# Attention's column input read from row-order images by strided matmul operands, instead of a second, column-order copy written by the first convolution

## What is computed

```python
B, H, W, C = (16, 56, 56, 64); NH = 8; KD = C // NH
x = x + dwconv3x3(x, pos_w, pos_b)
y = layernorm(x, ln1_g, ln1_b)
q = y @ q_w + q_b;  k = (y @ k_w + k_b) * KD ** -0.5;  v = y @ v_w + v_b
lepe = dwconv5x5(v, lepe_w, lepe_b)
attn_w = softmax(einsum('bhqnd,bhknd->bhnqk', qh, kh) + mask_w)     # along each image row
vw = einsum('bhnqk,bhknd->bhnqd', attn_w, vh)
attn_h = softmax(einsum('bqwnd,bkwnd->bwnqk', qh, kh) + mask_h)     # along each image column
out = einsum('bwnqk,bknwd->bqwnd', attn_h, vw)
x = x + (out + lepe) @ out_w + out_b
x = x + gelu(layernorm(x, ln2_g, ln2_b) @ fc1_w + fc1_b) @ fc2_w + fc2_b
```

## Time and profile before

| | |
|---|---|
| median of three runs | 2081.37 us |
| the profiled execution | 2082.95 us; its span 2081.2 us |
| first convolution | 0 to 297 us of the span |
| attention, rows; columns | 297 to about 935; to about 1535 us |
| second convolution; MLP | about 1535 to 1775; to 2081 us |
| busy, share of the span | PE 89%, PE weight loads 74%, DVE 69%, ACT 60%, POOL 53% |
| DMA | 346.85 MB, mean 167 GB/s |

### The profile page before, as it was taken

How to read it: one execution, slowest core, us unless ns; L and a number is a source line. 1 busy time by engine, 2 the same in 40 slices (tenths; PEclk the granted TensorE clock), 3 DMA queues, 4 the chain that set the end, 5 groups by cost and what they waited for, 6 DMA issues and landing times. The chain is left out here.

```text
span 2081.2 us, 89304 instructions
## 1 busy us (share of the span) xinstructions
PE 1844.1 (89%) x34510; PEld 1546.4 (74%) x34510; DVE 1432.1 (69%) x2285; ACT 1251.9 (60%) x2126; POOL 1111.3 (53%) x1904
## 2 busy tenths in 40 slices
PE   5887427999999999998999999999977886699998
PEld 5887424888887888876877878878867886577776
DVE  3698965777777777766776767767641655688885
ACT  4688754555555555564555555555543667588887
POOL 5357454555455554554555555545543001699997
PEclk8988756999999999999999999999988998799999
DMA  8689747778887787887777777777759995565553
GB/s 136 109 201 232 208 152 178 177 172 181 179 182 170 175 180 171 178 183 172 180 181 175 180 178 179 182 171 181 177 77 148 181 211 175 128 138 135 137 136 82
DMA packets 661155, 346.85 MB, mean 167 GB/s; under 512 B 562462, under 2 KB 613406, under 8 KB 660878
## 3 DMA queue, kind: packets, MB, share of 16 engines
q1 hardware_dynamic: 627782, 298.69, 66.7%
q0 software_dynamic: 31936, 43.83, 7.1%
q10 hardware_dynamic: 1160, 0.13, 0.0%
HBM read 105.42 MB, written 102.76 MB: 100 GB/s over the span
## 5 line engine op out<-in xcount | busy, mean ns | idle before, releaser
L917 ACT ACTIVATE att_prob<-att_st_ps 128x448 f32<-128x448 f32 x896 | 487.0, 544 | 436.9 <-PE att_st_ps L825 436.8
L993 DVE TENSOR_REDUCE att_mm<-att_s_ps 128x8 bf16<-128x448 f32 x896 | 555.9, 621 | 269.1 <-PE att_s_ps L795 265.6
L838 PEld LDWEIGHTS att_pv_ps<-att_vx,att_prob 128*56 128x56 f32 x14336 | 562.3, 132 | 88.0 <-ACT att_prob L917 4.7
L838 PE MATMUL att_pv_ps<-att_vx,att_prob 128*56 128x18 f32 x14336 | 514.6, 202 | 5.2 <-ACT att_prob L917 3.3
L687 POOL DMA_DIRECT2D att_mvt<-att_mneg x256 | 135.8, 535 | 559.1 <-ACT att_mneg L906 476.0
L820 PE MATMUL att_st_ps<-att_mvt,set_both 122*56 122x448 bf16 x1792 | 345.9, 357 | 15.4 <-DMA att_mvt<-att_mneg 14.7
L795 PE MATMUL att_s_ps<-att_kx,att_q_unit 120*56 120x448 bf16 x1792 | 347.4, 360 | 6.9 <-DMA att_q_unit<-att_qk_hi 4.2
L825 PE MATMUL att_st_ps<-att_qx,att_k_hi 128*56 128x448 bf16 x1792 | 344.8, 356 | 0.0
L825 PE MATMUL att_st_ps<-att_qx,att_k_lo 128*56 128x448 bf16 x1792 | 342.4, 353 | 0.0
L678 POOL DMA_DIRECT2D att_qx<-att_q_hilo x512 | 245.1, 487 | 6.0 <-DMA att_q_hilo<-att_qk_lo 4.3
L900 ACT ACTIVATE att_qk_hi<-att_pj,set_bias 128x392 bf16<-128x392 f32 x256 | 150.2, 587 | 124.7 <-PE att_pj L753 124.6
(11 more groups left out here) (213 smaller groups left out, 3161.4 us busy)
## 6 DMA issues: line engine op xcount, KB each, us to landing
att_xt<-xn_chunks SPq DMA_DIRECT2D x128, 196.0 KB
att_k_hi<-att_qk_hi SPq DMA_DIRECT2D x128, 196.0 KB, 3.4
att_qx<-att_q_hilo POOLq DMA_DIRECT2D x512, 49.0 KB
att_k_lo<-att_qk_lo SPq DMA_DIRECT2D x128, 196.0 KB, 3.9
pos_x<-in_x_dram SPq DMA_DIRECT2D x128, 105.0 KB
lepe_x<-v_scratch SPq DMA_DIRECT2D x128, 105.0 KB, 4.4
x_scratch<-pos_x SPq DMA_DIRECT2D x128, 98.0 KB
xn_chunks<-pos_xrt SPq DMA_DIRECT2D x16, 784.0 KB, 5.2
```

What stands on the lines that cost most here:

```text
L838: ins = pe.matmul(pv_ps[v % 2][64 * h:64 * h + L, at:at + 18], prob[t % 4][:, 4 * h + a, :], vx[v][:, VW * j + 36 * a + 18 * h:VW * j + 36 ...
L917: act.activation(out, src, ACT.Exp).then_inc(exp_done, 1)
L993: dve.tensor_reduce(mm[v % 2][:, NH * j:NH * j + NH], s_ps[j % 2][:, 0:S8].rearrange("p (s k) -> p s k", k=L), AX.X, ALU.max).then_inc(max ...
```

## The change

Four things are changed.

1. The first convolution writes no column-order copy: `xct`, its four DVE copies and its store per image are gone. The four row copies of an image are split: ACT makes the first two (`ACT_G = 2`), DVE the other two (`row_copy(n, g)`), where the column copies stood. `hl` has three buffers instead of two.
2. Attention's columns load row-order images: four DMAs of 196 KB fill an image `xi` (two buffers), the DMAs of an image are issued nine and ten chunks ahead in the SP stream (before: five and six), and `project` reads 7 columns of the image as an operand of 56 runs of 7 elements, 56 elements apart. The projection then lies in PSUM with the token's place in its column outermost, so `high` and `low` read PSUM with a step of 7 elements, and write as before.
3. SP's stream of attention is written out instead of looped.
4. At attention's start `load_x(i, 3)` goes ahead of the queries' copies on SP, and on POOL the clearing of the second `qx` goes ahead of filling the first.

The diff, cut:

```diff
+        xi = [sb(f"xi{u}", [128, H, W], BF16) for u in range(2)]
...
+        def by_line(i, t):
+            if i.rows:
+                return t[:, 0:HALF].rearrange("p (l q) -> p l q", q=L)
+            return t[:, 0:HALF].rearrange("p (q l) -> p l q", q=L)
...
+                wait(sp, v_proj, cnt(p, pv, 1, 1))
+                sp.dma_start(xt[u][:, :], x_d[4 * i.at + v]).then_inc(xt_in[u], 16)
+            def load_image_rows(i, v):
+                u = i.at % 2
+                if i.at >= 2:
+                    sp.wait_ge(qk_proj, cnt(Image(i.at - 2, False), 3, 2, 2))
+                sp.dma_start(xi[u][:, LINES * v:LINES * v + LINES, :].rearrange("p l q -> p (l q)"),
+                             x_d[4 * i.at + v]).then_inc(xi_in[u], 16)
+            def load_ahead(i, v, d):
+                near, far = chunk(i, v, d), chunk(i, v, d + 4)
+                if near[0].rows:
+                    load_x(*near)
+                if not far[0].rows and is_there(*far):
+                    load_image_rows(*far)
...
-            loop(sp, body, first)
+            straight(sp, body, first)
...
-                x = xt[v % 2][:, HALF * th:HALF * th + HALF]
+                if i.rows:
+                    x = xt[v % 2][:, HALF * th:HALF * th + HALF].rearrange("p (a b) -> p a b", b=PAIRS)
+                else:
+                    first_line = LINES * v + PAIRS * th
+                    x = xi[i.at % 2][:, :, first_line:first_line + PAIRS]
...
-                act.activation(qk_hi[w][:, at:at + HALF], pj[th][:, 0:HALF], ACT.Identity,
+                act.activation(qk_hi[w][:, at:at + HALF].rearrange("p (l q) -> p l q", q=L), by_line(i, pj[th]), ACT.Identity,
...
-        HL = 2 if pos else 3
+        HL = 3
+        ACT_G = G // 2 if pos else G
...
-                for g in range(G):
+                for g in range(ACT_G):
                     s, jj = g // 2, g % 2
                     act.wait_ge(tr_done, G * n + g + 1)
...
+            def row_copy(n, g):
+                s, jj = g // 2, g % 2
+                if n >= 2:
+                    dve.wait_ge(xr_out[n % 2], 16 * (n // 2))
+                dve.wait_ge(tr_done, G * n + g + 1)
+                rows = xrt[n % 2][:, :, :].rearrange("p g (l q) -> p (g l) q", q=W)
+                dve.tensor_copy(rows[:, 28 * jj:28 * jj + 28, WH * s:WH * s + WH], turned(G * n + g)).then_inc(xr_dve, 1)
...
-                        col_copy(n - 2, range(0, 2))
+                        row_copy(n - 2, 2)
                     variance(n)
...
-                        col_copy(n - 2, range(2, G))
+                        row_copy(n - 2, 3)
```

More of the change, by code:

```diff
@@ L395, in attention_phase @@
         xt_in = [sem(f"xt_in{u}") for u in range(2)]
+        xi_in = [sem(f"xi_in{u}") for u in range(2)]
         kx_in = [sem(f"kx_in{w}") for w in range(2)]
@@ L537, in load_x @@
                 p, pv = chunk(i, v, -2)
-                if p.rows:
-                    wait(sp, v_proj, cnt(p, pv, 1, 1))
-                else:
-                    wait(sp, qk_proj, cnt(p, pv, 2, 2))
-                sp.dma_start(xt[u][:, :], x_d[4 * i.n + v]).then_inc(xt_in[u], 16)
+                wait(sp, v_proj, cnt(p, pv, 1, 1))
[12 more added lines that the diff above has]
+                    load_image_rows(*far)
             def load_v(i, v):
@@ L603, in first @@
                 load_x(i, 2)
+                load_x(i, 3)
                 queries(i, 0)
@@ L622, in body @@
                 w = v // 2
-                n2, n3, n4, n5, n6 = (chunk(i, v, d) for d in (2, 3, 4, 5, 6))
+                n2, n3, n4 = (chunk(i, v, d) for d in (2, 3, 4))
                 if v % 2 == 0:
@@ L752, in project @@
                         cs = slice(C * c, C * c + C)
-                        ins = pe.matmul(pj[th][cs, 0:HALF], w[:, cs], x, start=part == 0, stop=part == 1)
+                        ins = pe.matmul(pj[th][cs, 0:HALF].rearrange("p (a b) -> p a b", b=PAIRS), w[:, cs], x,
+                                        start=part == 0, stop=part == 1)
                 ins.then_inc(qk_proj, 1)
@@ L1094, in conv_phase @@
             sq = sb("sq", [128, NBLK, C], F32)
-            xct = [sb(f"xct{u}", [128, W, H], BF16) for u in range(2)]
             st = [sb(f"st{u}", [128, 4, NBLK], F32) for u in range(2)]
@@ L1143, in conv_phase @@
         xr_out = [sem(f"xr_out{u}") for u in range(2)]
-        xc_out = [sem(f"xc_out{u}") for u in range(2)]
         no_x = sem("no_x")
@@ L1276, in _ @@
             if pos:
-                for u in range(2):
-                    sp.wait_ge(xc_out[u], 16 * B // 2)
                 for q in range(NB4):
@@ L1665, in _ @@
                 scale(B - 1)
-                col_copy(B - 2, range(G))
-                col_copy(B - 1, range(G))
+                for n in (B - 2, B - 1):
+                    for g in range(ACT_G, G):
+                        row_copy(n, g)
 def mlp_phase(nc, setup, rt_d, x1_d, out_d):
@@ L2030, in build @@
         conv_phase(nc, "lepe", False, v_d, lepe_w.rearrange("a b o c -> a b (o c)"), lepe_b, att_d,
-                   None, rt_d, None, mlp=after)
+                   None, rt_d, mlp=after)
         mlp_phase(nc, after, rt_d, x1_d, out)
```

59 lines of the change are left out of this document (23 added, 36 removed).

## The result

| | before | after |
|---|---|---|
| median | 2076.56 us (7 runs) | 2066.29 us (7 runs) |
| ratio after/before | | 0.9931, 95% interval 0.9918 to 0.9945 |
| profiled execution; its span | 2082.95; 2081.2 us | 2067.62; 2065.4 us |
| attention's first load | 297.26 us | 278.14 us |
| fourth transposition of maxima | 362.80 us | 345.99 us |

What follows compares the result with a forecast made beforehand. PE was taken to bound attention; in the first convolution DVE, or for images 4 to 7 the transfers and their queue. Terms 3.5 + 9.3 + 7 + 7 + 2 + 3 + 7 = 38.8 us gave 2043 us, range 2026 to 2068.

Steps and rivals of the forecast that it cites:

- step 6: Attention's columns, projection on PE: reading the operand in 56 runs of 7 costs nothing, 0 us, within bounds 0 to 18.
- Step 1: First convolution, images 2, 3, 8 to 15: DVE's two row copies for four column copies save 1.77 us per image.
- step 2: First convolution, images 4 to 7: without column stores, transfers and SP queue take 12.5 us per image, saving 9.3 us.
- step 4: Attention's start: loading the fourth chunk's input ahead of the mask rows saves 3 us, between 0 and 9.
- the five signs: DVE period 9.2–9.8 us, SP queue period 11.5–13.5, first load about 268, no column wait for input, projection half 0.33 us.
- 3. end of the convolution: End of the first convolution: the row store is now last and lands with nothing beside it, 2 us less.
- Step 5: Attention's columns: PE's six waits for a chunk's input vanish because images are issued nine and ten chunks ahead, 7 us less.
- the first convolution does not follow: Rival: copies' time passes to the ACT and POOL chain, SP's queue stays at 15.1 us; 2060 us, chance 0.09.
- The bound of 18 us: Attention's columns, projection: upper bound if breaks between runs cost all of L825's 0.01 us reading error, 0.14 us per half.
- the waits only move: Rival: in attention PE next stops for the maxima's transfer or keys, input-wait and start gains give nothing; 2053 us, chance 0.10.
- Step 7: Attention's columns: `high` and `low` reading PSUM with a step of 7 floats costs nothing.

## Why the prediction was wrong

The sign of the whole was right and the time fell into its range, but only because that range was wide; its sum of 38.8 us was some 2.5 times too large. Four of its terms failed. The largest is step 6: the projection was put at nothing and cost 10 us. Step 1 gave 5.7 us less than forecast, step 2 gave 4.1 less, and step 4 had the wrong sign. Of the five signs that it named, one came, PE's wait for input gone from the columns; the other four missed, at 10.7 us per image, 13.8 us of queue per image, a first load at 278 us and 0.42 us per half. By its own steps, in the profiled executions:

| step | forecast | measured |
|---|---|---|
| 1. images 2 and 3 | -3.5 | -2.3 (images 1 to 3) |
| 2. images 4 to 7 | -9.3 | -5.2 |
| 1. images 8 to 11 | -7 | -5.3 |
| 1. images 12 to 15 | -7 | -4.2 |
| 3. end of the convolution (with 1.0 up to image 0) | -2 | -2.2 |
| 4. attention's start | -3 | +2.3 |
| 5. waits for input in the columns | -7 | -7.0, with +1.6 of waits for maxima |
| 6. projection | 0 | +10 |

The measured terms of attention after its start add up to +4.6 us (steps 5 and 6); the transpositions of maxima in the two traces say +3.8.

*Step 1*, the copies. I took the upper price of a copy and with it left the chain aside, because 9.12 us was under DVE's 9.8. The copy in fact took 0.47 us, about half of 0.885. The Trainium skill, "VectorE: DVE Perf Modes", section "Mode 2×_1P", has two elements per cycle for 16-bit data with step 1; I had weighed that and set it aside, and the trace agrees with it. DVE's work fell to 9.1 us, but the chain that I had read as 9.12 us from the trace before did not stay 9.12. Its inverse had stood beside a DVE operation that reads one tensor; with DVE faster it came to stand beside centring, which reads two, and grew from 1.6 to 3.2 us. Here the step failed: I compared the engine's new load with a chain measured under the old overlap. POOL's part of the chain, named in the rival "the first convolution does not follow", was the right place to look. Images 8 to 15 gave 9.5 us, 1.2 each, between that rival's 0.8 and the forecast's 1.77; the longer inverse is in neither.

The behaviour itself, as the runs here show it, is that an operation of POOL and one of DVE with two operands in SBUF don't run at once: the second waits for the end of the first (1.89 us in place of 0.24; 4.91 in place of 2.0; 0.72 in place of 0.19). The Trainium skill says this in "SBUF — State Buffer", section "Who interferes with whom", of GpSimd operations that read SBUF and of VectorE operations with two SBUF inputs, and that the one issued first goes on; these rows agree. The prediction could have used it and did not.

*Step 2*, the transfers. They give 10 us in the run without the column store, but only 4 of them up to image 7. The SP queue's period in images 4 to 7 is 13.8 us, not 12.5: eight stores of the convolved image issue in 6.5 us, between the 4.6 of a quiet queue and the 8.1 of the earlier trace rows, and the loads still wait for their landing. ACT's wait for a landed row store went only from 11.2 to 10.1 us:

```profile
122.61 4.38 SPq L1248 DMA_DIRECT2D pos_x<-in_x_dram  x8
...
127.52 6.50 SPq L1262 DMA_DIRECT2D x_scratch<-pos_x  x8
136.26 5.01 SPq L1248 DMA_DIRECT2D pos_x<-in_x_dram  x8
...
163.91 3.86 SPq L1248 DMA_DIRECT2D pos_x<-in_x_dram  x8
```

```profile
ACT pos_xrt L1509 <- DMA xn_chunks<-pos_xrt: 10.1, 3, 3.9
```

*Step 4* had the sign wrong. The load of the fourth chunk ahead of the masks saves its own wait and makes the next ones longer; undone, about 3 us come back by the fourth transposition (the +2.3 of the table is between two single traces). I had counted the wait that goes and not what is late next, the second unit's queries.

*Step 6* is the largest failure: the four halves shown have a mean of (0.39 + 0.46 + 0.45 + 0.38) / 4 = 0.42 us. All the halves that the two traces have (125 and 128) have a mean of 0.422 us after and 0.343 before (the 0.33 of the earlier trace rows was one of the shortest), which is 10 us by 128 halves. L825, whose runs are 112 bytes long, could not show it. The bound of 18 us from that row's reading error held; the value 0 inside it was not supported. *SBUF — State Buffer*, section "Door 1: The DMA port swizzle", in the Trainium skill pointed the right way with its lines of 16 bytes, and the runs agree on the 16 bytes. It asks for two hits per line; here it took about four elements of 2 bytes, and even a run of 7 within one line was not free, and so the 1.5 to 5 us that I had estimated by it became 10.

*Step 5* held as such: no wait for the input is left. Part of it may have come back at the maxima, as the rival "the waits only move" had it: 8.8 us against 7.2, and 8.5 to 12.2 in ten traces with the changed kernel's column code, against a single trace before.

*Step 7* held: ACT's eviction takes 0.587 us and DVE's 0.626 with either step.

## What to carry to other kernels

- Before a chain is compared with an engine's new load, look which operations will then stand beside each other. An operation of POOL and one of DVE with two operands in SBUF exclude each other, so that a faster DVE can make a POOL step eight times as long; the chain's length is a property of the overlap, not of its operations.
- When an operand of TensorE becomes strided, count the pieces of 16 bytes per run, not the runs. Here splitting the same work into 14 columns by 28 rows in place of 7 by 56 took the projection's extra cost from 10 to 3 us, and the total fell by 8.6.
- Moving one step of a ring needs the program order of every engine in it. Two of the orders tried made the kernel 16 to 22 us slower than the change and one, with ACT's order mended as well, 8 us faster.

## What the runs showed of the hardware

- A projection of four matmuls with 392 columns takes 0.33 us from neighbouring elements, 0.38 from runs of 7 within 16 aligned bytes, 0.45 where 1 or 2 of the 7 lie beyond a 16-byte edge, and 1.36 us from single elements 16 bytes apart. Runs of 8, 14 and 28 from an aligned start are free, and so is an odd start of one long run.
- DVE's copy of 128x784 bf16 from PSUM takes 0.47 us in row order and 0.885 us with rows and columns exchanged.
- In the columns PE's wait for the maxima recurs in nearly every trace at the same places, about 1083, 1231 and 1380 us in the changed kernel, and with it the sum of the last 59 intervals scatters from 542 to 550 us among ten traces whose column code is the same. What causes it was not tried. A scatter of 8 us is enough to hide a gain of 3 us at the start; that it is also why the parts don't quite add up is a guess.
